# Attention in a two-layer graph kernel: the negated row maxima of two key tiles enter the scores in quarters of the TensorE array, and the PSUM ring runs in another order

## What is computed

```python
sx = einsum('bsh,ndh->bnsd', x, hl_w) + hl_b          # 4 heads n of 64
q = einsum('bnsd,neod->bneso', sx, wq)                # 4 experts e per head
k, v = sx @ wk, sx @ wv
scores = einsum('bnesd,bntd->bnest', q, k) * 8 + causal
att = softmax(scores)                                 # over the keys t
qkv = einsum('bnest,bntd->bnesd', att, v)
out = qkv of the 4 experts side by side
gs = softmax(out @ gate_w + gate_b)                   # a gate over the experts
mixed = sum over e of qkv[e] * gs[e]
```

## Time and profile before

| what | value |
|---|---|
| median of 3 runs | 3468.97 us (3467.27 to 3474.9) |
| the profiled execution's own time | 3469.29 us |
| its span, first to last instruction | 3467.6 us |
| mean granted TensorE clock | 0.937 of full speed |
| attention stage, about | 1126 to 3310 us of the span |
| TensorE matmul busy | 3079.7 us, 89% of the span |
| VectorE, ScalarE, GpSimd busy | 1757.7, 1236.7 and 1862.6 us |

### The profile page before, as it was taken

How to read it: one execution, slowest core, us unless ns; L and a number is a source line. 1 busy time by engine, 2 the same in 40 slices (tenths; PEclk the granted TensorE clock), 3 DMA queues, 4 the chain that set the end, 5 groups by cost and what they waited for, 6 DMA issues and landing times. The chain is left out here.

```text
span 3467.6 us, 46110 instructions
## 1 busy us (share of the span) xinstructions
PE 3079.7 (89%) x18162; PEld 1862.0 (54%) x18162; DVE 1757.7 (51%) x2797; ACT 1236.7 (36%) x1637; POOL 1862.6 (54%) x992
## 2 busy tenths in 40 slices
PE   7999987689998889999999999788999999999943
PEld 3445656377875555555555555455555555555422
DVE  4522764487833455565555640155656565563056
ACT  2210320356531233334444344233343434434423
POOL 0000020333310356778788899546677879889924
PEclk9999888899998799999999999789999999999966
DMA  9951100399950000000000000000000000000001
GB/s 392 424 207 46 60 1 8 110 295 272 261 94 15 1 1 1 1 1 1 1 1 1 1 1 1 1 1 1 1 1 1 1 1 1 1 1 1 1 4 40
DMA packets 63748, 195.36 MB, mean 56 GB/s; under 512 B 8243, under 2 KB 25137, under 8 KB 53554
## 3 DMA queue, kind: packets, MB, share of 16 engines
q1 hardware_dynamic: 38786, 148.11, 11.1%
q0 software_dynamic: 24752, 44.31, 7.1%
HBM read 188.99 MB, written 3.41 MB: 55 GB/s over the span
## 5 line engine op out<-in xcount | busy, mean ns | idle before, releaser
L1866 POOL TENSOR_TENSOR at_acc<-at_acc,at_pt 128x1024 f32<-128x1024 f32 (+3 forms) x728 | 1556.9, 2139 | 277.9 <-ACT at_pt L1702 194.7
L1762 DVE TENSOR_REDUCE at_mx<-at_psR 128x2 f32<-128x1024 f32 (+3 forms) x784 | 858.6, 1112 | 854.2 <-PE at_psR L1593 539.4
L1702 ACT ACTIVATE at_pt<-at_psR 128x1024 f32<-128x1024 f32 (+3 forms) x784 | 731.1, 936 | 991.5 <-PE at_psR L1614 607.3
L1630 PE MATMUL at_psO<-at_pt,v 128*64 128x512 f32 (+3 forms) x3136 | 702.7, 569 | 15.8 <-DVE at_oT L1781 10.6
L1611 PE MATMUL at_psR<-at_qhi,at_klo 64*128 64x512 f32 (+3 forms) x1568 | 345.9, 436 | 58.7 <-ACT at_pt L1702 27.5
L1630 PEld LDWEIGHTS at_psO<-at_pt,v 128*64 128x64 f32 x3136 | 193.1, 138 | 338.2 <-issue 277.2
L1593 PE MATMUL at_psR<-at_khi,at_qhi 64*128 64x512 f32 (+3 forms) x1568 | 341.9, 430 | 33.7 <-ACT at_pt L1702 9.4
L1246 PE MATMUL ga_acc<-h,ga_ring 128*128 128x257 f32 (+1 forms) x1352 | 305.3, 386 | 29.8 <-ACT ga_ring L1140 26.3
L1611 PEld LDWEIGHTS at_psR<-at_qhi,at_klo 64*128 64x128 f32 x1568 | 152.1, 188 | 328.9 <-issue 306.2
L1611 PE MATMUL at_psR<-at_qlo,at_khi 64*128 64x512 f32 (+3 forms) x1568 | 300.8, 377 | 0.0
L1611 PE MATMUL at_psR<-at_qhi,at_khi 64*128 64x512 f32 (+3 forms) x1568 | 300.1, 376 | 0.0
(11 more groups left out here) (318 smaller groups left out, 3276.8 us busy)
## 6 DMA issues: line engine op xcount, KB each, us to landing
gc_rows<-in_adj SPq DMA_DIRECT2D x26, 1664.0 KB, 17.3
ga_rows<-in_adj SPq DMA_DIRECT2D x26, 1664.0 KB, 9.9
ga_ring<-in_adjT POOLq DMA_DIRECT2D x78, 512.0 KB, 23.7
gc_cols<-in_adjT SPq DMA_DIRECT2D x26, 1024.0 KB, 15.1
gc_ring<-in_adjT SPq DMA_DIRECT2D x26, 512.0 KB, 7.6
gc_ring<-in_adjT SPq DMA_DIRECT2D x13, 256.0 KB, 2.8
ga_ring<-in_adjT POOLq DMA_DIRECT2D x13, 256.0 KB, 9.2
out_x<-X SPq DMA_DIRECT2D x6, 512.0 KB
```

Of the source, the lines that this page charges most:

```text
L1630: ins = pe.matmul(psO[lanes[l], off:off + w], v1[:, t, (2 * hp + l) * D:(2 * hp + l + 1) * D], pt[:, g % PTS, l, 0:w], start=g == FIRST[u] ...
L1702: act.activation(pt[:, g % PTS, :, 0:w], psR[:, slot_of["score", g] % SLOTS, :, 0:w], ACT.Exp).then_inc(e_ready, 1)
L1762: dve.tensor_reduce(mx[:, u % 2, :, s, c:c + 1].rearrange("p l o -> p (l o)"), psR[:, slot_of["max", i] % SLOTS, :, 0:w], AX.X, ALU.max).t ...
L1866: pool.tensor_tensor(to, to, got, ALU.add).then_inc(added, 1)
```

## The change

Four edits.

1. `negm` has one buffer of 97 columns in place of two of 65; `maxima` writes each lane's negated maximum twice, at columns 0 and 32 for lane 0 and 64 and 96 for lane 1 (its input is read twice by a broadcast), and now waits for the turn of the unit before. `row_of_maxima` turns and copies 97 columns.
2. The pass L1614 leaves `scores`. A new function `less_maxima` does it ahead of the products, for both tiles of a step at once: four products of 32 rows each, in four quarters of the array's rows, into four banks. It takes the slots of both tiles, so it waits for both.
3. In a step TensorE's order becomes: `less_maxima` of both tiles, first piece, scores of both tiles (three passes each), other pieces, turns, values.
4. The ring's order becomes piece, score, score, other pieces. The second piece of a step thus has the slot of the first piece of that step.

```diff
+QUAD = 32
 def slot_users():
-            for half in range(2):
-                if g + 2 + half < FIRST[NU]:
-                    out.append(("score", g + 2 + half))
-                out += [("max", piece[0]) for piece in max_pieces(u, k, half)]
+            pieces = [("max", piece[0]) for half in range(2) for piece in max_pieces(u, k, half)]
+            out += pieces[:1] + [("score", x) for x in (g + 2, g + 3) if x < FIRST[NU]] + pieces[1:]
...
-        negm = m.sb("at_negm", [P, 2, SUB, D + 1])
+        negm = m.sb("at_negm", [P, SUB, 3 * QUAD + 1])
+        quads = [[slice((2 * l + i) * QUAD, (2 * l + i + 1) * QUAD) for l in range(2)] for i in range(2)]
...
-                        ins = pe.transpose(psX[0:D + 1, s * P:(s + 1) * P], negm[:, u % 2, s, :], ident[:, :])
+                        ins = pe.transpose(psX[0:3 * QUAD + 1, s * P:(s + 1) * P], negm[:, s, :], ident[:, :])
...
+                def less_maxima(g):
+                    u = GROUPS[g][0]
+                    pe.wait_ge(x_read, turn_of["r", u] + 1)
+                    slots = [take_slot(pe, ("score", g + i)) for i in range(2)]
+                    for i in range(2):
+                        _, t, off, w = GROUPS[g + i]
+                        for l in range(2):
+                            pe.matmul(psR[:, slots[i], l, 0:w], ones_r[quads[i][l], :],
+                                      nm[quads[i][l], u % 2, off:off + w], start=True, stop=False)
+
                 def scores(g):
-                    pe.wait_ge(x_read, turn_of["r", u] + 1)
-                    slot = take_slot(pe, ("score", g))
+                    slot = slot_of["score", g] % SLOTS
-                    for l in range(2):
-                        ins = pe.matmul(psR[:, slot, l, 0:w], ones_r[lanes[l], :], nm[lanes[l], u % 2, off:off + w],
-                                        start=False, stop=not diag)
...
-                        for half in range(2):
-                            if g + 2 < ng:
-                                scores(g + 2 + half)
-                            for piece in max_pieces(u, k, half):
-                                row_max(u + 2, *piece)
+                        if g + 2 < ng:
+                            less_maxima(g + 2)
+                        pieces = max_pieces(u, k, 0) + max_pieces(u, k, 1)
+                        for piece in pieces[:1]:
+                            row_max(u + 2, *piece)
+                        if g + 2 < ng:
+                            scores(g + 2)
+                            scores(g + 3)
+                        for piece in pieces[1:]:
+                            row_max(u + 2, *piece)
...
-                    if u >= 2:
-                        dve.wait_ge(x_full, turn_of["r", u - 2] + 1)
+                    if u >= 1:
+                        dve.wait_ge(x_full, turn_of["r", u - 1] + 1)
...
-                        ins = dve.tensor_reduce(negm[:, u % 2, s, 0:D + 1:D], mx[:, u % 2, :, s, 0:seen], AX.X, ALU.max, negate=True)
+                        ins = dve.tensor_reduce(negm[:, s, 0:3 * QUAD + 1:QUAD].rearrange("p (l i) -> p l i", i=2),
+                                                mx[:, u % 2, :, s, 0:seen].unsqueeze(2).broadcast_to([P, 2, 2, seen]),
+                                                AX.X, ALU.max, negate=True)
```

More of the change, by code:

```diff
@@ L1604, in scores @@
                     hp, b, e = UNITS[u]
-                    pe.wait_ge(x_read, turn_of["r", u] + 1)
-                    slot = take_slot(pe, ("score", g))
+                    slot = slot_of["score", g] % SLOTS
                     kc = key_column(hp, t)
                     diag = t * P >= QBLOCKS[b][0]
-                    for left, right, first in ((klo, qhi, True), (khi, qlo, False), (khi, qhi, False)):
+                    for left, right, last in ((klo, qhi, False), (khi, qlo, False), (khi, qhi, True)):
                         for l in range(2):
-                            pe.matmul(psR[:, slot, l, 0:w], left[lanes[l], kc:kc + P],
-                                      right[lanes[l], u % 3, off:off + w], start=first, stop=False)
-                    for l in range(2):
-                        ins = pe.matmul(psR[:, slot, l, 0:w], ones_r[lanes[l], :], nm[lanes[l], u % 2, off:off + w],
-                                        start=False, stop=not diag)
+                            ins = pe.matmul(psR[:, slot, l, 0:w], left[lanes[l], kc:kc + P],
+                                            right[lanes[l], u % 3, off:off + w], start=False, stop=last and not diag)
                     if diag:
@@ L1645, in _ @@
                 queries(2)
+                less_maxima(0)
                 scores(0)
@@ L1681, in row_of_maxima @@
                     act.wait_ge(x_full, turn_of["r", u] + 1)
-                    act.activation(nm[0:D + 1, u % 2, 0:bw], psX[0:D + 1, 0:bw], ACT.Copy).then_inc(x_read, 1)
+                    act.activation(nm[0:3 * QUAD + 1, u % 2, 0:bw], psX[0:3 * QUAD + 1, 0:bw], ACT.Copy).then_inc(x_read, 1)
                 def turn_out(u, h):
@@ L1874, in gate @@
                             2).broadcast_to([P, ws * NE * 2, D]), ALU.mult).then_inc(weighed, 1)
-                pool.memset(negm[:, :, :, :], 0.0).then_inc(zeros, 1)
+                pool.memset(negm[:, :, :], 0.0).then_inc(zeros, 1)
                 pool.memset(nm[:, :, :].bitcast(F32), 0.0).then_inc(consts, 1)
```

## The result

The changed kernel takes **3538.84 us** (median of 4 runs, 3537.36 to 3545.3) against 3469.17 before: ratio 1.0207, 95% interval 1.0194 to 1.0221. It is 70 us slower. The forecast was slower by 35: the sign and the mechanism held, the size was half.

The account below looks back on a forecast made before the run. TensorE was taken as the bound, its regular step fixed by the second piece's start, with GpSimd setting the pace in block 6. Terms -28 + 19 + 5 + 30 + 4 + 5 = +35 gave 3504 us, range 3455 to 3545.

Parts of the forecast that it names:

- the mechanism: Each step's second piece waits for VectorE's reduce of the first piece, no longer for an exponential; chain 1.80 to 1.91 us.
- First steps of a unit: Blocks 1 to 5: second piece 0.48 us later, behind VectorE's output, `negm` and reduce; 40 steps, 19 us lost.
- Diagonal steps: Wider one gains 0.32 us, narrow one loses 0.44, as scores between the pieces shrink; 40 x 0.12, 5 us lost.
- Block 6: GpSimd sets the pace and hides all but the gate stretch's loss ahead of unit 25: 2 x 2.5, 5 us lost.
- the quarters start within 0.01 us of each other: Rival in `less_maxima`: quarters run in pairs (3544 us) or one by one (3636 us) instead of together; chance 0.10.
- GpSimd's lag: Rival in gate stretches: GpSimd sets those units' length, so the 30 and 5 us losses go; 3469 us, chance 0.13.
- 1.99: Faster rival, second piece of each step: six passes cover the reduce, so it starts at 1.99 us; about 3454 us, chance 0.21.
- the gate stretches: TensorE waits where VectorE computes gates: 2.9 us for each of eight units, 2.2 for three lesser; 30 us lost.
- The regular steps: Blocks 1 to 5: second piece at 2.17 to 2.28 us instead of 2.41; 148 x 0.19, 28 us gained.
- the turn of `negm`: Four products turning 97 columns instead of 65, 0.027 us more each in 40 units: 4 us lost.
- 3513: Total in us if switching quarters to halves costs in full: regular steps gain 0.13 instead of 0.19, 9 us more.
- three lesser ones at 2.2: Gate units in blocks 0 and 1, each taken to lose 2.2 us, within the 30 us for gates.

Follow-up runs that it names:

- e2: Changed kernel with ring and TensorE order back at score, piece, score, other pieces, quarters of `less_maxima` kept at the step's head: 3542.92 us, ratio 1.0222.
- e5: Kernel before with e4's order only in steps 1 to 2b-2 of blocks 2 to 6 (expert 0 without steps 3 to 6): 3414.01 us, ratio 0.9844.
- e6: Changed kernel with VectorE's sum over the experts and its addition to `hn` left out of the third gate piece: 3472.49 us.
- e11: Changed kernel with the third gate piece in two parts, a step apart, all work kept: 3509.6 us, ratio 1.0126.
- e4: Kernel before with ring and TensorE order piece, score, score, other pieces; halves inside the scores, no `less_maxima`: 3470.83 us, ratio 1.0006.
- e9: e3 with `less_maxima` in two passes of halves instead of one of four quarters: 3485.67 us, ratio 1.0055.
- e1: Changed kernel with halves instead of quarters in `less_maxima` and no second copy of the negated maxima: 3535.64 us, ratio 1.0205.
- e3: Changed kernel with the first piece ahead of `less_maxima` in TensorE's queue, ring and quarters as changed: 3526.71 us, ratio 1.0176.
- e10: e5 with the third gate piece split in VectorE's queue in units of 7 steps and more: 3406.51 us, ratio 0.9823.
- e8: Changed kernel with the values ahead of the second piece in step 5 of 8 units (expert 0, blocks 3 to 6): 3537.61 us, ratio 1.0201.

## Why the prediction fell short

**The mechanism held.** The chain from the first piece to the second was read as 1.80 to 1.91 us and measures 1.92 (1886.36 to 1888.28). First steps of a unit: 19 forecast for 40, 12.0 measured for 30 of them. Diagonal steps: 5 forecast for 40 pairs, 10.9 - 5.9 = 5.0 measured for 28 and 26 steps, so the exact hit is luck. Block 6 stayed with GpSimd in experts 2 and 3, and of the rivals none came: the quarters start within 0.01 us of each other, GpSimd's lag swallowed none of the gates of blocks 3 to 5, and the second piece of a regular step stood at 2.36 us, not at 1.99. That the ring makes the loss in the gate stretches is shown by e2 and e5 (old order there, loss mostly or wholly gone) and by e6 and e11 (same order, VectorE's work shorter or cut in two). The ring alone isn't a loss as a whole: e4 has its order and stands level with the kernel before. The changed kernel lacks the gain of e4's regular steps because `less_maxima` stands ahead of the first piece; e9 against e1 shows that.

**Where the missing 35 us are.** The regular steps gave 14 us less than forecast, the gate stretches cost 13 more, block 6 cost 7 more, and block 0 cost 10 without a term of its own; the first steps and the turn of `negm`, forecast too dear, take back some 10.

**Term mis-sized: the regular steps, 28 forecast, about 14 given.** The step that failed is the place of the second piece, forecast at 2.17 to 2.28 us and measured at 2.36, and in it "0 to 0.11, I take half, 0.05" for the switch between halves and quarters. `less_maxima` holds the queue for 0.44 where the prediction had 0.26 + 0.11 = 0.37, and the reduce starts the full 0.55 after the piece, so that the chain is 1.92 where I took the middle of 1.80 to 1.91. In the one step shown that leaves 0.05 us of gain where I had 0.19; over these rows it is 0.10 a step, and they are 140 steps, not 148. Here the measurement sides with the rule that I had set beside the row: the Trainium skill, TensorEngine Tiling (Array Packing), section Tiling Modes, says that a change of mode drains TensorE; the 0.43 of e3 for a pass that is 0.23 among halves fits it. I had 3513 by it, and even that priced the way out alone.

**Term mis-sized: the gate stretches, 30 forecast, 43 measured.** A block's stretch costs 4.5 us in blocks 3 to 5 (26.8 for 6), not 2.9. The hole was forecast right ("over 5", 5.47), and so was the delay of the first gate piece (1.2; that step takes 5.93 instead of 4.71). The step that failed is that what the clock does behind the hole was "left to the range" and had no price in the sum: values of 3.61 us instead of 1.87 are the missing part. And block 1, put among "three lesser ones at 2.2", costs 6.0 in each head pair: in its second unit the gate's work delays the first piece of two successive short steps, each with a wait of its own (1.71 us at 1201.88 and 3.31 at 1211.64 in the first pair) and half clock behind it, and the two steps are 3.65 and 3.67 us longer. I had read the row of one block and carried it to the others by a guess.

**Term mis-sized: block 6, 5 forecast, 12.3 measured.** I let GpSimd's lag take up part of the gate's delay there. Steps 3 to 6 of expert 0, the gate stretches of the two pairs, are 5.1 and 5.4 us longer, a little more than in blocks 3 to 5. With the gate split in two (e11) they are 0.2 longer and 0.2 shorter, and the whole block is 3.0 longer.

**Block 0, 9.7 us, had no term of its own** beyond the lesser gates. What differs there is the clock: its seven steps spent 102 us at 1.2 GHz after the change and 81 before, and half of those 21 us is about the loss. The row follows the clock in the other runs too (e3 80 us and -0.3, e9 105 us and 7.4), also where the code is the same (e5 74 us and -1.8, e10 99 us and 4.7). So how much of it is the change's doing and how much differs from execution to execution stays open.

**A small term too large:** turning 97 columns instead of 65 takes 0.61 against 0.58 us for four (1752.79 to 1753.40 against 1730.38 to 1730.96), under 2 us in sum where I had 4.

## What to carry to other kernels

A ring of buffers decides which engine each user waits for; moving a user by one place can swap a wait on a fast, punctual reader for one on an engine with other work in its queue. Price such a wait not in the regular step, where it may be a draw, but wherever that engine is late, and add the half clock behind each hole. When an order wins in one kind of step and loses in another, use both: here, without the quarters, that turned an order level with the old one (e4, 1.0006) into a gain of 1.6% (e5), and of 1.8% with the gate split (e10).

## What the runs showed of the hardware that I had not expected

- Four products of 32 rows and 512 columns run together in 0.51 us, yet hold TensorE's queue for 0.43 to 0.44 where a pass of two products of 64 rows takes 0.23; the passes on either side take 0.34 and 0.43 instead of 0.24 and 0.34 (e3 against e9). In this kernel a quarter pass is worth nothing beside two half passes.
- After 5.47 us without a matmul, all value products of the step ran at half clock (1.2 GHz, 3.61 us). In e8, after 3.64 us without one, one pass at full clock and 1.41 us more without one, the next step had 0.58 of full clock over 6.95 us. In e11, after 2.29 us without one, a step's quarters still took 0.80 us instead of 0.51. Before the change, 2.64 us without one was followed by 0.71 of full clock over the 5.93 us from 1760.96.
